# Attention scores of a Trainium2 kernel: from the whole TensorE array for one head to 32 array rows for each of four heads

## The reference

```python
b, s = 2, 1024;  E, H, D = 128, 16, 8
v = x @ w_v + v_b
q = (x @ w_q + q_b) @ w_k.T + k_b        # keys are x itself
scores = einsum('bhqd,bhkd->bhqk', qh, kh) / sqrt(8)
scores = where(causal, scores, finfo.min)
probs  = softmax(scores);  out = einsum('bhqk,bhkd->bhqd', probs, v) @ c_proj_w + c_proj_b
```

## Time and profile before

| | us |
|---|---|
| median of 3 runs | 560.67 (558.43 to 560.69) |
| the profiled execution's own time | 556.93 |
| its span in the trace | 555.1 |
| one body of the loop (six of them) | 29.5 |
| body of group 6, body of group 7 (from first PV to first PV, and to the last out) | 26.9, 24.9 |
| granted TensorE clock, mean | 0.98 |

### The profile page before, as it was taken

One profiled execution on the slowest core, in us unless ns is written; L12 is line 12 of the kernel. 1 busy time (PEld: TensorE's weight loads), 2 busy tenths in 40 slices (PEclk: granted clock), 3 DMA queues, 4 the chain that ended last, 5 costly groups with the idle time before them and its releaser, 6 DMA issues.

```text
span 555.1 us, 11378 instructions
## 1 busy us (share of the span) xinstructions
PE 516.0 (93%) x3574; PEld 402.7 (73%) x3574; DVE 386.5 (70%) x1013; ACT 319.7 (58%) x678; POOL 273.0 (49%) x417
## 2 busy tenths in 40 slices
PE   5988879999988899999999999999999889899995
PEld 2888869988845556656565656666656889899994
DVE  5786735557489787979797887978554776545744
ACT  4563434458344767767676776767776444444643
POOL 8399888767484502131211112020418888864440
PEclk9999999999987899999999999999999999999998
DMA  8932424232859723132140505030001041441314
GB/s 282 295 85 53 113 72 122 58 106 82 236 156 217 237 49 126 54 102 80 51 130 2 179 1 180 0 104 2 2 2 35 31 93 44 107 112 58 120 39 119
DMA packets 41384, 54.65 MB, mean 98 GB/s; under 512 B 6064, under 2 KB 32176, under 8 KB 40560
## 3 DMA queue, kind: packets, MB, share of 16 engines
q1 hardware_dynamic: 31664, 41.13, 26.4%
q0 software_dynamic: 4480, 9.25, 5.0%
q10 hardware_dynamic: 5184, 3.55, 2.2%
...
## 4 chain that ended last, share of the span: by engine, by line
PE 64%; POOL 15%; DVE 8%; DMA 5%; issue 4%; ACT 1%; ACTq 1%; SPq 0%; POOLq 0%; DVEq 0%
PE psum L1654 13%; PE psum L1611 12%; PE psum L1683 11%; POOL z_rows L1184 10%; PE psum L943 7%; PE psum L929 3%; POOL idle L1194 3%; PE psum L909 3%; PE psum L910 3%; PE psum L911 3%; DVE mxp L1764 3%; PE psum L1614 2%; DMA b_p<-in_attn_c_proj_b 2%; PE psum L1639 1%; PE psum L963 1%
## 5 line engine op out<-in xcount | busy, mean ns | idle before, releaser
L1764 DVE TENSOR_REDUCE mxp<-psum 128x1 f32<-128x512 f32 (+3 forms) x304 | 179.3, 654 | 34.4 <-PE psum L1611 30.6
L1823 ACT ACTIVATE probs<-psum 128x512 f32<-128x512 f32 (+1 forms) x304 | 155.3, 578 | 32.2 <-PE psum L1654 29.2
L1654 PE MATMUL psum<-queries,keys 128*128 128x512 f32 (+3 forms) x384 | 123.4, 383 | 2.9 <-DMA queries<-m_rows 2.5
L1872 POOL TENSOR_SCALAR_AFFINE_SELECT probs<-probs 128x512 f32<-128x512 f32 x64 | 40.1, 637 | 172.0 <-ACT probs L1823 171.9
L1611 PE MATMUL psum<-keys,queries 128*128 128x512 f32 (+1 forms) x304 | 116.7, 421 | 2.3 <-DVE mxp L1764 1.7
L1010 ACT ACTIVATE silu<-psum 128x352 f32<-128x352 f32 x107 | 49.6, 464 | 96.2 <-PE psum L911 95.3
L1053 DVE TENSOR_TENSOR act<-silu,psum 128x352 f32<-128x352 f32 x107 | 55.5, 519 | 65.7 <-ACT silu L1010 64.6
L1207 POOL DMA_INDIRECT y_rows<-ys,to_row x76 | 74.2, 976 | 50.6 <-DVE ys L1089 30.3
L943 PE MATMUL psum<-wall_f,at 128*128 (+1 forms) x648 | 91.3, 277 | 1.9 <-DVE x L1091 1.3
L1654 PEld LDWEIGHTS psum<-queries,keys 128*128 128x128 f32 x384 | 67.3, 192 | 28.6 <-ACT probs L1823 12.4
L943 PEld LDWEIGHTS psum<-wall_f,at 128*128 128x128 f32 x648 | 81.5, 193 | 2.8 <-ACT at L1018 1.7
...
## 6 DMA issues: line engine op xcount, KB each, us to landing
...
queries<-q_stack SPq DMA_DIRECT2D x8, 512.0 KB, 6.1
...
keys<-q_stack SPq DMA_DIRECT2D x4, 512.0 KB, 11.4
...
```

The lines of the kernel that those rows point to most:

```text
L1654: ins = e.matmul(slot(K, u, d, n)[:, m * (q1 - q0):(m + 1) * (q1 - q0)], K.keys[v][:, j, kt * P:(kt + 1) * P], K.queries[v][:, q0:q1], sta ...
L1764: e.tensor_reduce(K.mxp[:, heads[0]:heads[-1] + 1, i, which], scores, AX.X, ALU.max).then_inc(K.A["taken"], 1)
L1823: e.activation(probs_of(K, product)[:, heads[0]:heads[-1] + 1, :], src, ACT.Exp, scale=SCALE).then_inc(K.A["ex"], 1)
```

## The change

- `keys` becomes [128, 1024]: head j's keys in partitions 32j to 32j+31, no zeros. `wipe_pool` and `keys_clear` go. A group's keys are loaded by one DMA of 512 KB in place of four of 128 KB. Where POOL wiped between two scatters it now does its usual pause memset.
- Every score matmul reads 32 partitions of both operands, the head's own, so it uses 32 of the array's rows. A bank holds scores of one head only. The ring has 40 units of one head (before 38), with two query tiles in a bank where they are narrow. There are 40 exponential units (before 38), by strips of the keys; two narrow strips get a tile of their own (`probs_narrow`).
- The causal mask is written first (`mask_pe`, K in the strings): four bf16 matmuls into 32 partitions each of the bank, 128 or 256 columns wide; the score matmul then adds to it (start=False). There are 24 K in a group. K waits for the bank in place of its R.
- New order strings; `AHEAD` 10 becomes 12, `LEAD` 14 becomes 22; PV products and masks in another order.

The core of the diff:

```diff
-        runs.append((i, i, 1, (0, 1, 2, 3), 0))
-        for n, k0 in enumerate(range(0, i, TPC)):
...
+    whole = [[(i, 0, TPC)] for i in range(TPC, KT)]
+    diagonal = [[(3, 0, 4)], [(7, 4, 4)], [(2, 0, 3)], [(6, 4, 3)], [(1, 0, 2), (5, 4, 2)], [(0, 0, 1), (4, 4, 1)]]
+    kinds = whole + diagonal
+    return [(kinds[k], j) for k in MAX_ORDER for j in range(4)]
+MAX_ORDER = (1, 2, 0, 3, 6, 7, 8, 4, 5, 9)
...
+STRIPS = [[0], [1, 2], [3], [4], [5], [6], [7], [8], [9, 10], [11]]
+UNITS = [(w, j) for w in range(len(STRIPS)) for j in range(4)]
-AHEAD = FIRST_UNIT[3]
-LEAD = 14
+AHEAD = 12
+LEAD = 22
...
-ORDERS = ['RURUURURURRaaaaRURURRRUURRaURURURURUURRURURURaaURRURURURURUURURUURaaaaaRURURURURRURURURURUUR', ...
+ORDERS = ['KKRUURKaKKURRUURaKKKURRURUaaKKRURURKKRURUaKKUURRKKURURKKUURRRURaRUUURRRRURRUaRURRUUaURRUaUURRaRURURUKaKURRUKKRRUUKKaURRU', ...
...
-                K.keys = [None, sb("keys1", [P, 4, SEQ], F32R, scope=s3), None]
+                K.keys = [None, sb("keys1", [P, SEQ], F32R, scope=s3), None]
...
-    ins = e.matmul(dst, K.queries[u][:, i * P:(i + 1) * P], K.keys[u][:, heads[0]:heads[-1] + 1, k0 * P:(k0 + nb) * P],
-                   start=True, stop=True, skip_group_check=True)
-    if which == 0:
-        ins = e.matmul(dst, K.mask_b[:, :], K.ident_b[:, :].unsqueeze(1).to_broadcast([P, len(heads), P]), start=False,
+    for i, k0, nb in parts:
+        ins = K.nc.tensor.matmul(bank(K, r_bank)[:, start:start + nb * P], K.queries[u][head_rows(j), i * P:(i + 1) * P],
+                                 K.keys[u][head_rows(j), k0 * P:(k0 + nb) * P], start=not masked(n), stop=True,
+                                 skip_group_check=True)
...
+def mask_pe(K, n, r, r_bank):
+    e, parts = K.nc.tensor, MAXES[n][0]
+    if r >= len(RING):
+        e.wait_ge(K.A["taken"], r + 1 - len(RING))
+    nb = parts[0][2]
+    for c in range(4):
+        dst = bank(K, r_bank)[head_rows(c), 0:len(parts) * nb * P].rearrange("p (a k) -> p a k", k=nb * P)
+        e.matmul(dst[:, :, (nb - 1) * P:], K.mask_b[:, head_rows(c)],
+                 K.ident_b[:, :].unsqueeze(1).to_broadcast([P, len(parts), P]), start=True, stop=True,
...
-    for m, j in enumerate(heads):
-        ins = e.matmul(slot(K, u, d, n)[:, m * (q1 - q0):(m + 1) * (q1 - q0)],
-                       K.keys[v][:, j, kt * P:(kt + 1) * P], K.queries[v][:, q0:q1], start=True, stop=True)
+    for product in STRIPS[w]:
+        kt, half = PRODUCTS[product]
+        q0, q1 = query_range(kt, half)
+        ins = e.matmul(slot(K, u, d, n)[:, at0:at0 + q1 - q0], K.keys[v][head_rows(j), kt * P:(kt + 1) * P],
+                       K.queries[v][head_rows(j), q0:q1], start=True, stop=True, skip_group_check=True)
```

More of the change, by code:

```diff
@@ L167, in width, with strip_width, units_for, freed_by @@
     return q1 - q0
[L170 to L173 removed]
+STRIPS = [[0], [1, 2], [3], [4], [5], [6], [7], [8], [9, 10], [11]]
+STRIP_OF = [w for w, products in enumerate(STRIPS) for _ in products]
+UNITS = [(w, j) for w in range(len(STRIPS)) for j in range(4)]
 NU = len(UNITS)
[L175 removed]
 DIAGONAL = [PRODUCTS.index((kt, kt // TPC)) for kt in range(KT)]
[L179 to L210 removed]
+MASK_ORDER = sorted(range(KT), key=lambda kt: DIAGONAL[kt])
+def strip_width(w):
+    return sum(width(*PRODUCTS[n]) for n in STRIPS[w])
+def units_for(n):
+    return 4 * (STRIP_OF[n] + 1)
+PROBS = 4 * CHUNK
+WIDE = [w for w in range(len(STRIPS)) if strip_width(w) == CHUNK]
+NARROW = [w for w in range(len(STRIPS)) if strip_width(w) < CHUNK]
+def freed_by(w):
+    at, among, ring = (WIDE.index(w), WIDE, PROBS // CHUNK) if w in WIDE else (NARROW.index(w), NARROW, len(NARROW))
+    before = among[(at - ring) % len(among)]
+    return STRIPS[before][-1] + 1 - (NPV if at < ring else 0)
+NARROW_WIDTH = CHUNK // 2
+FREED_BY = [freed_by(w) for w in range(len(STRIPS))]
+AHEAD = 12
+LEAD = 22
+MT_LATER = 3
+OUT_AT = (10, 24)
 def ring_of_body(nxt, nxt2):
@@ L218, in ring_of_body @@
     ring += b[MT_LATER:]
-    ring.insert(min(len(ring), 34), ("out", 0, 0))
+    ring.insert(min(len(ring), OUT_AT[1]), ("out", 0, 0))
     return ring
@@ L1645, in unit_pe @@
     e = K.nc.tensor
-    kt, half, heads = UNITS[n]
-    v = (u + d) % 3
+    w, j = UNITS[n]
+    v, at0 = (u + d) % 3, 0
     if not start:
@@ L1661, in slot, with strip_of @@
     return bank(K, SLOTS[((u + d) * NU + n) % 3])
+def strip_of(K, w):
+    if w in WIDE:
+        at0 = 4 * CHUNK * (WIDE.index(w) % (PROBS // CHUNK))
+        place = K.probs[:, at0:at0 + 4 * CHUNK]
+    else:
+        place = K.probs_narrow[:, NARROW.index(w), :]
+    return place.rearrange("p (j q) -> p j q", j=4)
 def probs_of(K, n):
-    at, size = 4 * PROBS_AT[n], 4 * width(*PRODUCTS[n])
-    return K.probs[:, at:at + size].rearrange("p (j q) -> p j q", j=4)
+    w = STRIP_OF[n]
+    at0 = sum(width(*PRODUCTS[m]) for m in STRIPS[w] if m < n)
+    return strip_of(K, w)[:, :, at0:at0 + width(*PRODUCTS[n])]
 def pv_pe(K, p, u, n):
@@ L1692, in pe_body @@
     units = [(0, n) for n in range(AHEAD, NU)] + ([(1, n) for n in range(AHEAD)] if kind != LAST else [])
+    masks = [k for k, (kind_of, _, n) in enumerate(ring) if kind_of == "max" and masked(n)]
     for what in ORDERS[kind]:
@@ L1697, in pe_body @@
             kind_of, dd, n = ring[took]
+            assert took not in masks
             number = count(p, u, RINGN, RING0[kind] + took)
@@ L1700, in pe_body @@
             took += 1
+        elif what == "K":
+            k = masks.pop(0)
+            number = count(p, u, RINGN, RING0[kind] + k)
+            mask_pe(K, ring[k][2], number, RING[number % len(RING)])
         elif what == "E":
@@ L1703, in pe_body @@
         elif what == "W":
-            awake_pe(K, p, u, units[0][1] if units else NU + 1)
+            awake_pe(K, p, u, units[0][1] if units else NU + 3)
         else:
             pv_pe(K, p, u, products.pop(0))
-    assert took == len(ring) and not early and not units and not products
+    assert took == len(ring) and not early and not units and not products and not masks
 def awake_pe(K, p, u, n):
-    K.nc.tensor.wait_ge(K.A["ex"], count(p, u, NU, n - 2))
+    K.nc.tensor.wait_ge(K.A["ex"], count(p, u, NU, min(n - 2, NU)))
     busy_pe(K, slot(K, u, 0, n))
@@ L1744, in attn_pe @@
             unit_pe(K, 0, 0, 0, r - UNITS_FROM, start=r - UNITS_FROM < 3)
-        ring_pe(K, what, d, n, 0, 0, r, RING[r % len(RING)], start=r < len(RING))
+        if what == "max" and masked(n):
+            mask_pe(K, n, r, RING[r % len(RING)])
+        ring_pe(K, what, d, n, 0, 0, r, RING[r % len(RING)])
     for n in range(len(RING_PROLOGUE) - UNITS_FROM, AHEAD):
```

143 lines of the change are left out of this document (53 added, 90 removed).

## The result

The changed kernel takes 575.0 us (median of 4 runs, 573.17 to 576.89), the kernel before 560.7 beside it (4 runs, 558.43 to 565.59): 1.024 times, 95% interval 1.017 to 1.032. The forecast was 551 us, range 535 to 582: the time lies in the range, but a gain of 10 us was forecast and 14 us were lost. The profiled execution took 574.49 us.

The account below looks back on a forecast made before the run. PE was taken to bound the loop before the change, DVE after it. Six bodies -16.8, prologue +4, group 6 +2 and group 7 +1 sum to -9.8 us; 560.67 - 9.8 gives 551 us, range 535 to 582.

Parts of the forecast that it names:

- A body of 26.7 us: Loop: each body falls from 29.5 to 26.7 us, DVE's 24.9 plus 1.8 of waits; six bodies -16.8 us.
- rival 2: Score matmuls on different array rows do not overlap; +41 us, 602 us; chance 0.08.
- rival 3: Loop: DVE waits 4.5 us a body as before; +6 us, 567 us; chance 0.12.
- Changes between rows and columns at 0.165 us: PE: each change of form costs 0.165 us, 0.33 a round trip; 35 a loop body in place of 8, 5.8 us.
- Rival 1: A change between rows and columns costs twice as much, 0.33 us; +20 us, 581 us; chance 0.17 together with the clock rival.
- Prologue +4: Before the first loop body: further entries, fewer waits and the clock together add 4 us, ends +1 and +12.
- That is level at 2.4 GHz, not at 1.2 ... I add 1.6: Prologue: a masked unit's PE time about matches DVE's 0.59 us at full clock only; 1.6 us added for clock falls.
- The further entries: Prologue: 64 entries before the first body instead of 54; ten more reductions of 0.59 us, +5.9, less 2 and 1.5.
- Rival 5, the clock: Loop: rarer full streams let the clock fall to 1.2 GHz, nearly doubling PE's 22.4 us; small, within 0.17 shared with rival 1.
- Group 6 +2: Group 6: 29 us against 26.9 before, with 41 changes of form for 10; +2 us, ends -1 and +4.
- Group 7 +1: Group 7: 28 changes of form for 16, rows saving 3.6 us, PV waiting for whole strips; +1 us, ends -2 and +3.
- Edits at nothing: POOL's wipes turned pauses, `keys_clear` removed, single key DMA, FFN 2: 0, at most -1 us for `keys_clear`.

Follow-up runs that it names:

- e12: Changed kernel with the last ten ring entries before the first loop body taking maxima over 16 keys only; 575.8 us, 1.019 times the kernel before.
- e14: Kernel before, with single-head score matmuls in its prologue on 32 array rows in place of 128; 571.1 us, 1.014 times the kernel before.
- e16: Kernel before, with small 32-row matmuls added in its prologue for the changes of form, score matmuls kept whole-array; 565.9 us, 1.008 times the kernel before.
- e1: Changed kernel plus four 32-column matmuls that compute nothing before every second prologue ring entry from the fifth; 590.5 us, 1.051 times the kernel before.
- e2: Changed kernel plus one 32-column matmul that computes nothing before every second prologue ring entry from the fifth; 587.8 us, 1.039 times the kernel before.
- e3: Changed kernel with group 0's 24 masks in the prologue laid two at a time; 566.2 us, 1.005 times the kernel before.
- e17: Changed kernel with new orders of entries in groups 6 and 7 alone; 566.0 us, 1.007 times the kernel before.
- e5: Changed kernel plus two to four 32-row matmuls that compute nothing behind every prologue score matmul from the fifth; 577.5 us, 1.027 times the kernel before.

## Why the prediction was wrong, point by point

- *A body of 26.7 us*: 26.15 measured, six bodies -18.0 for -16.8. Rows overlap (rival 2 falls), DVE waits 1.4 us a body for the 1.8 taken (rival 3 falls).
- *Changes between rows and columns at 0.165 us* held at full clock (a body has 36 changes of form and had 10, for the 35 and 8 taken): in the loop's rows 0.17 us from mask to score (275.26 to 275.43) and 0.44 from score to PV (275.43 to 275.87). Less the mask's stream (0.06, the step from 0.17 to the 0.23 of two masks, 276.75 to 276.98) and the score's 0.23 that is 0.32 a round trip, an estimate, for the 0.33 taken. Rival 1 falls as stated; at half clock a round trip cost 0.41.
- *Prologue +4*: +16.5, beyond its end of +12. This is the step that failed, and in it the sentences "That is level at 2.4 GHz, not at 1.2 ... I add 1.6". The working saw that the clock fell in this place and that a masked unit then exceeds DVE, and still priced the clock as the kernel before had it, 14 us long; the change itself lengthened it to 56. The further entries were not the miss: from `nmax`, behind which eight of the ten stand, to the first PV it was +1.4, for the +5.9 - 2 - 1.5 = 2.4 of all ten, and e12 got back 0.7. Between the two profiles compared above, -9.8 forecast and +12.9 measured are 22.7 us apart: 12.5 of them are the prologue's, 9.3 those of groups 6 and 7.
- *Rival 5, the clock*, was called small by counting PE's streams in time (15.5 of 26.7 us). e14 and e16 show that the array's share counts too. It also named the wrong place, the loop, which held at 1.0 in the profile of after to within 3.2 us of its end. In e1, e2, e3 and e17 the clock fell once to three times in the loop: by POOL's copies of v one body of e17 is then 28.04 us, the one before it 26.61 and the others 26.14. So the loop is close to it.
- *Group 6 +2*: +5.5, beyond its end of +4; its 29 us was right at full clock (e5). *Group 7 +1*: +6.8, beyond its end of +3, with the clock at 0.68 over it, and mended by another order. It is the same step again: both were priced at full clock.
- *Edits at nothing*: FFN 1 and 2 moved no more than the kernel before does by itself.
